# Issuing the store and the loads of 1/sum from SyncE in a two-layer local-attention kernel

## The reference

```python
sim = jnp.where(mask, -jnp.finfo(sim.dtype).max, sim)
attn = jax.nn.softmax(sim, axis=-1)
out = jnp.einsum('bhwij,bhwjd->bhwid', attn, bv)
...
x = x + o @ wo
```

## Time and profile before

| | before |
|---|---|
| median of 3 runs | 2815.74 us (2815.32 to 2817.94) |
| profiled execution, its own time | 2814.85 us |
| its span | 2812.7 us |
| PE busy | 2657.1 us, 94% of the span |
| DVE busy | 2312.4 us, 82% |
| ACT busy | 2295.3 us, 82% |
| POOL busy | 1618.1 us, 58% |
| mean granted TensorE clock | 0.983 of full speed |
| DMA queues | q1 (issued by SP) 127.82 MB, q10 (issued by ACT) 34.10 MB |

### The profile page before, as it was taken

The page is one execution under the profiler, slowest core; times in us unless marked ns, Lnnn a source line. Parts: engine busy times, 40 slices in busy tenths (PEclk is TensorE's granted clock), DMA queues, the critical chain, the costliest instruction groups (busy, mean ns, idle before and its releaser), DMA issues.

```text
span 2812.7 us, 81243 instructions
## 1 busy us (share of the span) xinstructions
PE 2657.1 (94%) x30148; PEld 2393.2 (85%) x30148; DVE 2312.4 (82%) x6461; ACT 2295.3 (82%) x5559; POOL 1618.1 (58%) x1652
## 2 busy tenths in 40 slices
PE   7999947899999999999999999999999999999998
PEld 6887846788888888888888888888888888888887
DVE  3989986988888889888888788888888888888874
ACT  4979965788888888888888787888888888888884
POOL 2323216666666666666666565666666666666653
PEclk9999978999999999999999999999999999999999
DMA  3252111111112221112111223111111111111111
GB/s 102 64 188 69 46 53 53 56 54 54 56 50 57 58 58 55 54 55 58 53 52 51 86 60 102 41 51 51 51 51 51 51 51 50 48 51 51 51 43 42
DMA packets 211355, 167.10 MB, mean 59 GB/s; under 512 B 21522, under 2 KB 206612, under 8 KB 209940
## 3 DMA queue, kind: packets, MB, share of 16 engines
q1 hardware_dynamic: 139284, 127.82, 15.0%
q10 hardware_dynamic: 71680, 34.10, 4.2%
HBM read 110.89 MB, written 42.58 MB: 55 GB/s over the span
## 4 chain that ended last, share of the span: by engine, by line
PE 62%; DVE 15%; ACT 12%; issue 6%; POOL 2%; DMA 2%; SPq 1%; ACTq 0%; DVEq 0%; POOLq 0%
PE ps L439 19%; PE ps L438 15%; PE ps L405 10%; PE ps L505 6%; PE ps L521 4%; ACT Sm L830 4%; DVE Sm L1215 3%; PE ps L537 3%; PE ps L490 2%; DVE ss L1191 2%; DVE Ar L1184 1%; PE ps L547 1%; DVE Gl L1287 1%; ACT PT L837 1%; ACT zf L876 1%
## 5 line engine op out<-in xcount | busy, mean ns | idle before, releaser
L830 ACT ACTIVATE Sm<-Sm,nb 128x256 f32<-128x256 f32 (+1 forms) x1024 | 503.0, 496 | 1.2 <-DVE nb L1215 0.4
L1215 DVE CUSTOM_DVE_ANT_0 Sm<-ps,mask,sc 128x256 f32<-128x256 f32 (+1 forms) x1024 | 422.3, 475 | 33.2 <-issue 26.5
L1393 POOL TENSOR_TENSOR rs<-rs,mhalf 128x8 f32<-128x8 f32 x256 | 423.5, 1654 | 6.6
L438 PE MATMUL ps<-zTh,W1h 128*128 128x256 f32 (+1 forms) x1408 | 372.4, 286 | 0.0
L438 PE MATMUL ps<-zTh,W1l 128*128 128x256 f32 (+1 forms) x1408 | 366.6, 282 | 0.0
L1481 POOL TENSOR_TENSOR uTl<-Gl,uTh 128x512 fp32r<-128x512 f32 (+1 forms) x192 | 212.9, 1117 | 267.2 <-ACT uTh L902 267.2
L1287 DVE SCALAR_TENSOR_TENSOR Gl<-ps,vecs,Gl 128x256 f32<-128x256 f32 (+1 forms) x384 | 173.6, 480 | 210.7 <-ACT Gl L894 123.6
L1492 POOL TENSOR_TENSOR Ar<-Ar,Br 128x512 f32<-128x512 f32 x128 | 165.0, 1289 | 313.3 <-DVE Br L1186 312.1
L439 PE MATMUL ps<-WQh,hTh 128*128 128x512 f32 x768 | 331.3, 431 | 0.4 <-DVE Gl L1287 0.4
L439 PE MATMUL ps<-WQl,hTh 128*128 128x512 f32 x768 | 304.9, 397 | 0.0
L438 PE MATMUL ps<-zTl,W1h 128*128 128x256 f32 (+1 forms) x1408 | 283.3, 283 | 0.0
(11 more groups left out here) (190 smaller groups left out, 8533.7 us busy)
## 6 DMA issues: line engine op xcount, KB each, us to landing
oF<-ro_scratch ACTq DMA_DIRECT2D x256, 128.0 KB, 3.0
tb<-tab SPq DMA_DIRECT2D x128, 128.0 KB, 2.3
xc<-x SPq DMA_DIRECT2D x32, 256.0 KB, 3.1
rwkv_scratch<-rw SPq DMA_DIRECT2D x32, 256.0 KB, 2.7
rk<-rwkv_scratch SPq DMA_DIRECT2D x64, 128.0 KB, 2.3
xin<-x SPq DMA_DIRECT2D x64, 128.0 KB, 2.3
x_scratch<-x SPq DMA_DIRECT2D x64, 128.0 KB, 1.7
y_scratch<-os SPq DMA_DIRECT2D x64, 128.0 KB, 4.1
```

The source lines that it names most:

```text
L438: return pe.matmul(dst, W(b, k), D(a, k), **flags)
L830: act.activation(Sm[:, h, c0:c1_], Sm[:, h, c0:c1_], ACT.Exp, bias=nb[:, h:h + 1], scale=-1.0, accum_out=sm[:, n % 2, h:h + 1]).then_inc(S ...
L1215: dve.tensor_tensor_reduce(Sm[:, h, c0:c1_], PS[:, bank["scores", n, q, h % 2], (h // 2 % 2) * 256 + c0:(h // 2 % 2) * 256 + c1_], mask[:, ...
L1393: return pool.tensor_tensor(ap, ap, mhalf[:, 0:ap.shape[-1]], ALU.pow)
```

## The change

`store_r` and `load_r` move, unchanged but for the engine, from ACT's program to SP's. ACT's program issued the store a little after `rT_out` and the loads after one group of exponentials (and on odd steps the copy of v). In SP's program both come one right behind the other, in every step, after `shift` and before the output stores, the reloads of `W2`, `W1` and `WQ`, the store of `x1` and the loads of `x1i`, `tb` and `y`. The reload of `WO` stands ahead of them. Nothing else changes: the same 128 stores and 256 loads move the same bytes.

```diff
--- before.py
+++ after.py
@@ ScalarE, even steps
                     if live(2):
                         square(t - 2, 0)
-                    if live(5):
-                        store_r(t - 5)
-                    if live(2):
                         v_out(t - 2)
                     if live(4):
                         exp(t - 4, 0)
-                    if live(5):
-                        load_r(t - 5)
                     if live(1):
                         hT_hi(t - 1)
@@ SyncE
+            def store_r(n):
+
+                w.wait_ge(S["rT"], n + 1)
+                w.wait_ge(S["on"], n - 3)
+                sp.dma_start(ro_d[n % 4], r8[0:8, n % 2, :]).then_inc(S[f"sro{n % 2}"], 16)
+
+            def load_r(n):
+                w.wait_ge(S[f"sro{n % 2}"], 16 * (n // 2 + 1))
+                w.wait_ge(S["oTl"], n - 1)
+                w.wait_ge(S["oTh"], n - 1)
+                for par in range(2):
+                    sp.dma_start(oF[64 * par:64 * par + 64, n % 2, :, :], ro_d[n % 4, par:8:2, :].unsqueeze(
+                        0).broadcast_to([64, 4, 128])).then_inc(S[f"lro{n % 2}"], 16)
@@ SyncE, the loop over t
                 if live(7):
                     shift(t - 7)
+                if live(5):
+                    store_r(t - 5)
+                    load_r(t - 5)
                 if live(12) and not odd:
                     store_out(t - 13)
                     store_out(t - 12)
```

More of the change, by code:

```diff
@@ L845, in rT_out @@
                 act.activation(r8[0:8, n % 2, :], PS[0:8, bank["rT", n], 0:128], ACT.Copy).then_inc(S["rT"], 1)
[L847 to L859, removed]
             def o_out(n):
```

## The result

The changed kernel takes **2798.99 us** (median of 4 runs, 2798.03 to 2800.78), the kernel before 2815.53 us beside it: a ratio of 0.9942, 95% interval 0.9924 to 0.9959, so 16.5 us less. The forecast was 2803 us with a range of 2797 to 2810. A second set of 5 runs of the same kernel (the last experiment) gave 2797.10 against 2811.87, a ratio of 0.9950 (0.9938 to 0.9962), 14.8 us less. The profiled execution took 2798.03 us, its span 2795.9.

The account below looks back on a forecast made before the run. PE, busy 94% of the span, was taken as the bound, so only its stalls and slow clock offered time. Terms 7.7 + 1.7 + 1.2 + 1.7 + 0.3 = 12.6 us gave 2803 us, range 2797 to 2810.

Parts of the forecast that it names:

- Step 65: At the reload of WQ: loads of 1/sum go ahead of the weights, DVE's and PE's stalls vanish; 7.7 us gained.
- The later WQ: At the first product with the new WQ: reload issued 2.0 us later, 0.2 us taken off, bounds nothing to 1.1.
- Step 75: At the reload of W2: loads go ahead of the weights, DVE's 2.86 and PE's 1.72 us idle; 1.7 us gained.
- Step 74: At the reload of W1: issued later, behind store and loads, with 1.9 to 6.2 us of cover; cost nothing.
- ACT's holds in layer 1: Where ACT's queue runs dry until the loads are issued, PE waits for exponentials; 1.2 us gained, bounds 0 and 2.4.
- The floor of 0.6 us per pair: In layer 1, PE's wait of 0.61 us from the order of DVE and ACT, claimed to stay.
- Rival D: In layer 1, ACT's stream also causes PE's 0.61 us waits at 26 pairs; 15.9 us more gained, 2787; 5%.
- The last steps: At the end, ACT's holds of 1.67 and 5.48 us go; 1.7 and 0.3 us gained.
- the loads all the same: At the last unit, output still needs the loads, about 3 us after issue; multiplication only a few tenths earlier.
- Rival A: Even steps of layer 1: store lands later on SP's queue, DVE and PE wait; slower, 2832; 8%.
- Rival C: Stall moves to the weights or something else holds PE at both places; 3.2 us left, 2812.5; 10%.

Follow-up runs that it names:

- e3: Kernel before, with store and loads of 1/sum moved to SP for units 124 to 127 alone; 2810.43 us, ratio 0.9990.
- e4: Kernel before, with store and loads of 1/sum moved to SP for all units but 60, 70 and 124 to 127; 2811.04 us, ratio 0.9991.
- e5: Changed kernel, but SP issues the reloads of WQ and W2 ahead of the same step's store and loads of 1/sum; 2812.52 us, ratio 0.9999.
- e7: Kernel before, with the copy of 127 rows of x2 to h split into 112 and 15 rows; 2805.94 us, ratio 0.9975.
- e8: Changed kernel, with the reload of WQ also waiting for the multiplication of unit 60; 2803.23 us, ratio 0.9970.
- e2: Kernel before, with store and loads of 1/sum moved to SP for units 60 and 70 alone; 2804.03 us, ratio 0.9964.
- e1: Kernel before, nothing moved to SP, the reloads of WQ and W2 also waiting for ACT's copy of v; 2804.76 us, ratio 0.9959.
- e11: Changed kernel run once more, unaltered; 2797.10 us against 2811.87 for the kernel before, ratio 0.9950.
- e6: Changed kernel, with the copy of 127 rows of x2 to h split into 112 and 15 rows; 2796.74 us, ratio 0.9941.
- e9: Changed kernel, with store and loads of 1/sum left on ACT for units 124 to 127 and the copy to h split; 2796.66 us, ratio 0.9944.
- e10: Kernel before, nothing moved to SP, reloads of WQ and W2 held back and the copy to h split; 2793.46 us, ratio 0.9937.

## Why the prediction was right

The mechanism held where most of the gain lies, at steps 65 and 75 and at the end. The sum did less well than the range: 16.5 us against 12.6, and 2799.0 lies below the forecast's own bounds of 2801 to 2805.5. These held two slips. The largest terms add to 7.9 + 1.7 + 2.4 + 1.7 + 2 = 15.7 us, so the lower bound is 2800. And 0.25 MB of 3 MB in 11.8 us is 1.0 us, of which the cover of 0.3 takes a part, so WQ would have been late by 0.7 us and not by 1.1. The measured time is inside the range only because its lower end, 2797, was drawn below what the terms give; no term stood for that, so this part is luck.

**Step 65, forecast 7.7, measured 7.8 in the two traces, but 6.4 in other executions.** The mechanism held in each part: DVE's 7.72 us and PE's 5.05 us are gone, and the clock does not fall. Its size was taken from one execution that was dearer than others. Four other executions with ACT's or a late store's stall at step 65 (e3, e4, e5, e7) need 41.80 to 42.10 us from unit 59 to 61, not 43.52; without it they need about 35.6. With the profile of before among them, and without e5, the mean gain is 6.7 us. The difference is the clock after the stall. This is e4, two windows in a row from the end of PE's stall of 4.91 us:

```profile
1573.70:1576.70 3.00, 3.00 (x25) 2.88 (x26) 2.09 (x7) 2.38 (x6) 1.67 (x2) 0.50 0.04 9
1576.70:1579.70 3.00, 3.00 (x43) 2.86 (x43) 1.54 (x5) 2.39 (x5) 0.85 (x2) 0.98 0.06 18
```

There the clock is at the 1.2 GHz level for about 3 us, in the profile of before for 6. The forecast had no bound for that, having only the one execution.

**The later WQ, forecast 0.2 us, bounds 0 and 1.1.** It was issued 1.9 us later (1558.80 - 1554.72 = 4.08 us after the end of ACT's copy, against 2.17 before), forecast 2.0. It landed at 1559.31 + 12.1 = 1571.4, and the first product with WQ started at 1571.54. The cover was about 0.1 us, forecast 0.3. e8 confirms that each us more would have been paid in full.

**Step 75, forecast 1.7, measured 2.8** (2.7 as the mean of before, e3, e4 and e7 against 35.6). The stall of 1.72 us was counted, not the smaller ones behind it: PE's wait of 0.4 us for DVE's Gl in this stretch, for one, has gone too.

**Step 74, forecast 0.** W1 went out 7.7 us later after the copy of unit 69 than before. Its second half, issued at 1718.72, landed 11.8 us later at 1730.5, 6.1 us ahead of the first product with it (1736.66): no wait of PE for W1 in the list.

**ACT's holds in layer 1, forecast 1.2, bounds 0 and 2.4.** The floor of 0.6 us per pair stayed: PE waits 16.0 us 24 times in layer 1 up to 2800 where it was 18.3 us 26 times, and up to 2700, ahead of the last steps, 16.0 where it was 16.8. From unit 76 to 122 the two traces differ by 0.1 us the wrong way. The forecast's example was read wrongly: at the place of ACT's 1.36 us and PE's 1.23 us ACT still stands for 1.23 us in the changed kernel, though it issues no loads, and PE for 0.97:

```profile
2007.45 0.39 ACT L802 ACTIVATE hTh<-ps 128x256 fp32r<-128x256 f32 x1 [1.23 <-issue]
```

So the hold itself was worth about 0.3 us there (36.21 us for the pair before, 35.96 after); ACT's gap before L798 is gone, but most of it came back before L802, the next copy. Over the executions the stretch takes 819.2 us with SP issuing (7 of them) and 819.9 with ACT (6), less than they scatter. What is at stake is a rare event, 2.4 us, as in e2 and e3, and no run tells the term from nothing. Rival D is out.

**The last steps, forecast 2.0, bounds to 3.7, measured 2.8** (138.8 as the mean of before, e1, e2 and e4; 136.0 of the changed kernel twice, e3, e5 and e8). The first term, ACT's hold of 1.67 us, is gone, and the copy of unit 126 comes 1.3 us earlier after that of unit 122. Of the second, taken at 0.3, 1.5 us came back: the copy of unit 127 is 2.1 us earlier, its multiplication 2.5 (means of the same executions). The chain in the forecast's own rows had said so, since the store's 4.07 us stand on it. The scatter of the end is for a good part the clock: behind PE's last wait it is at 0.50 for over 6 us in the changed kernel's first profile and in e8 (136.95 and 136.96 us), for 3 in e3, e5 and e11 (134.99 to 135.44). What is left there is a new wait that the forecast spoke of as "the loads all the same". The last unit in the changed kernel, SP and DVE:

```profile
2737.26 0.30 SPq L1627 DMA_DIRECT2D ro_scratch<-r  x1
2740.96 1.29 SPq L1634 DMA_DIRECT2D oF<-ro_scratch  x2
...
2744.93 0.69 DVE L1210 TENSOR_TENSOR oF<-oS,oF 128x512 f32<-128x512 f32 x1 [2.81 <-DMA oF<-ro_scratch]
```

**Rival A, the store landing later on SP's queue.** It did not come to pass as a rule: the store does stand behind the copy to h, 3.62 us by the median where quiet steps have 1.22, but that was so before. On ACT's own queue the store's last packet started 3.9 us after the issue by the median, in 20 of 29 even steps of layer 1 more than 3 us after it, and in 19 of these 20 behind the last packet of the copy on SP's queue (at unit 75, 1840.59 against 1840.57). The taking of turns on which this rival stood gave the store nothing there. From the store to the loads ACT took 4.6 us in these steps, and still 3.40 with the copy split (e7).

In single steps rival A did happen. In the changed kernel's first profile DVE waited 0.62 us for the loads in one ordinary step and the pair lasted 35.93 us. In e11, e5 and twice in e8 it waited 0.86 to 1.03 us, PE then 0.71 to 1.22 us, and the pair lasted 36.5 to 37.3 us. The first of e8, DVE and then PE:

```profile
1874.61 0.69 DVE L1210 TENSOR_TENSOR oF<-oS,oF 128x512 f32<-128x512 f32 x1 [1.03 <-DMA oF<-ro_scratch]
...
1877.92 0.39 PE L505 MATMUL ps<-kTh,qTh 64*128 64x256 f32 x2 [1.20 <-DVE os L1276]
```

It is not SP's alone: e1, where ACT issues, has the same once (1.01 and 1.24 us, 37.22 for the pair). None of the four executions with the copy split has it.

**Rival C**, and the rule of the Trainium skill that the forecast set against itself (DMA: Bandwidth & Descriptors, section "Issuing engines are not separate DMA queues"): e1 and e5 agree with the sharing that it states, but a gain of ACT's issue time alone, 2812.5 us, did not come; the order gave the larger part. ACT's relief (e4) is the lesser part of the gain.

**What stays open.** By place the change explains 6.7 + 2.7 + 0 + 2.8 = 12.2 us on the average, the medians say 16.5 and 14.8. In the traces 3.4 us lie ahead of unit 5, where the profiled execution of before ends 541.6 us after the start and the changed kernel 538.2 and 539.4. All 13 executions lie between 538.2 and 541.6 there, on both sides: 540.4 us as the mean of the 6 in which ACT issues in these steps, 539.7 of the 7 with SP. Of the 3.4 us 3.2 are already there at 440 us, ahead of the first unit, where no part of the change runs, so they read as scatter between executions. The median of before was itself 2815.5, 2813.9, 2813.6 and 2811.9 us in the four sets of runs, and slow pairs of steps and the clock at the end move single executions by 1 to 2.5 us each. Why the medians differ by 3 to 4 us more than the places explain isn't settled. The forecast's sum was good partly since an overpriced step 65 met an underpriced step 75 and end.

## What to carry to other kernels

A small load that somebody needs soon has to be handed over before a large transfer that nobody needs yet; which engine issues it matters less. One wait in front of the large transfer may be enough, and it should be no longer than needed: check the landing of the large one against its first use. A price that contains a stall and the clock after it wants more than one execution, and beside a small latency-bound transfer look for a neighbour whose row count doesn't spread over the DMA engines.

## What the runs showed of the hardware

- A store of 4 KB landed 1.22 us after its issue in quiet steps, 3.6 us behind a copy of 127 rows, and 8.7 us behind 3 MB of weights of the same queue (e5).
- With the split copy the store of unit 127 landed in 2.45 us on SP's queue behind the copies (e6), on ACT's own queue in 1.25 us (e7), but also in 1.61 (e9) and 2.72 (e10): a queue of its own is not told from scatter there.
- After stalls of PE of 4.6 to 5.05 us at step 65 the granted clock was 0.50, the 1.2 GHz level, for 3 us in four executions and for 6 in one. After PE's last wait for unit 127 it fell in twelve executions and not in one (e7, a wait of 1.32 us).
- A copy of 127 rows on SP's queue held the last packet of a 4 KB store on ACT's queue, too: 3.9 us after the issue by the median, 0.8 with the copy split (e7).
- Issuing a DMA from ACT cost nothing that can be told while exponentials were queued: pairs of steps last 35.62 us with it (before) and 35.60 without (e4).
